# Order of value weighting and high-part subtraction on TensorE in a cross-attention and expert kernel

## The reference

```python
def xattn(q, k, v):
    qh, kh, vh = proj(q, w_q, b_q), proj(k, w_k, b_k), proj(v, w_v, b_v)   # 16 heads of 16
    scores = einsum('bhqd,bhkd->bhqk', qh, kh) / sqrt(16)
    attn = softmax(scores, axis=-1)
    ctx = einsum('bhqk,bhkd->bhqd', attn, vh)
    return einsum('bsd,ed->bse', ctx.reshape(B, S, D), w_o) + b_o

x = x + xattn(layernorm(x), ctx_1024, ctx_1024)
x = x + experts(layernorm(x))      # router, top 2 of 8, silu(x @ gate) * (x @ up) @ down
```

## Time and profile before

| what | value |
|---|---|
| median of 3 runs | 978.39 us (977.79 to 980.58) |
| the profiled execution | 976.2 us |
| its span, first to last instruction | 974.4 us |
| PE busy in the span | 875.0 us, 90% |
| DVE busy | 621.6 us, 64% |
| ACT busy | 468.9 us, 48% |
| POOL busy | 290.0 us, 30% |
| mean granted clock of TensorE | 0.958 |

### The profile page before, as it was taken

One profiled execution on the slowest core, in us unless ns is written; L12 is line 12 of the kernel. 1 busy time (PEld: TensorE's weight loads), 2 busy tenths in 40 slices (PEclk: granted clock), 3 DMA queues, 4 the chain that ended last, 5 costly groups with the idle time before them and its releaser, 6 DMA issues.

```text
span 974.4 us, 32193 instructions
## 1 busy us (share of the span) xinstructions
PE 875.0 (90%) x12208; PEld 781.1 (80%) x12208; DVE 621.6 (64%) x1930; ACT 468.9 (48%) x891; POOL 290.0 (30%) x337
## 2 busy tenths in 40 slices
PE   2899789999999761799999999999999999999995
PEld 1667667777777541789999999999999999999995
DVE  7788858888988544457547447545745746544443
ACT  3677757788878551335335334333523534323321
POOL 5556643344343325012112112212211112211111
PEclk9998979999999775899999999999999999999999
DMA  4321123222224312152522522522332352222221
GB/s 136 112 57 42 60 66 90 67 85 65 89 67 147 104 45 95 51 180 35 162 56 44 152 53 37 160 33 52 103 88 56 66 152 35 33 33 34 33 33 17
DMA packets 69073, 73.57 MB, mean 75 GB/s; under 512 B 19725, under 2 KB 62811, under 8 KB 69019
## 3 DMA queue, kind: packets, MB, share of 16 engines
q1 hardware_dynamic: 44666, 32.94, 11.7%
q0 software_dynamic: 12944, 17.87, 10.7%
q10 hardware_dynamic: 11408, 22.06, 6.4%
HBM read 45.18 MB, written 26.39 MB: 73 GB/s over the span
## 4 chain that ended last, share of the span: by engine, by line
PE 50%; issue 6%; DMA 6%; DVE 3%; ACT 3%; POOL 1%; SPq 0%; POOLq 0%; another core or an unknown queue 0%; ACTq 0%; DVEq 0%
PE bank L483 11%; PE bank L485 11%; PE bank L484 11%; PE bank L681 5%; PE bank L683 5%; PE bank L682 5%; DMA raw<-expert_rows 4%; DMA expert_rows<-rows,slot_u 2%; PE bank L656 1%; POOL expert_rows L1388 1%; PE bank L544 1%; DVE h_full L1252 1%; ACT h_hi L830 1%; DVE h_lo L1258 1%; ACT pt_hi L758 1%
## 5 line engine op out<-in xcount | busy, mean ns | idle before, releaser
L483 PE MATMUL bank<-xg,e_hi 128*128 128x128 f16 x2176 | 372.7, 219 | 0.7 <-DVE xg L1229 0.6
L484 PE MATMUL bank<-xg,e_hi 128*128 128x128 f16 x2176 | 372.7, 219 | 0.0
L485 PE MATMUL bank<-xg,e_lo 128*128 128x128 f16 x2176 | 372.7, 219 | 0.0
L1419 POOL DMA_INDIRECT out<-y_sb,tok_row x68 | 113.4, 1668 | 466.0 <-DVE y_sb L1247 442.5
L483 PEld LDWEIGHTS bank<-xg,e_hi 128*128 128x128 f16 x2176 | 213.4, 98 | 2.0 <-issue 0.8
L484 PEld LDWEIGHTS bank<-xg,e_hi 128*128 128x128 f16 x2176 | 213.4, 98 | 0.8
L485 PEld LDWEIGHTS bank<-xg,e_lo 128*128 128x128 f16 x2176 | 213.4, 98 | 0.0
L828 ACT ACTIVATE g_act<-bank 128x512 f32<-128x512 f32 x136 | 81.3, 598 | 249.1 <-PE bank L485 230.2
L1252 DVE SCALAR_TENSOR_TENSOR h_full<-bank,g_act 128x512 f32<-128x512 f32 x136 | 94.0, 691 | 129.3 <-ACT g_act L828 121.6
L681 PE MATMUL bank<-e_hi,h_hi 128*128 128x256 f16 x544 | 148.4, 273 | 3.8 <-DVE h_lo L1258 3.8
L682 PE MATMUL bank<-e_lo,h_hi 128*128 128x256 f16 x544 | 148.3, 273 | 0.0
(11 more groups left out here) (175 smaller groups left out, 1766.2 us busy)
## 6 DMA issues: line engine op xcount, KB each, us to landing
raw<-expert_rows SPq DMA_DIRECT2D x68, 132.5 KB, 2.6
e_stage<-in_gate_w ACTq DMA_DIRECT2D x7, 1024.0 KB
e_stage<-in_up_w ACTq DMA_DIRECT2D x7, 1024.0 KB
e_stage<-in_down_w ACTq DMA_DIRECT2D x7, 1024.0 KB
expert_rows<-pads SPq DMA_DIRECT2D x8, 530.0 KB
xin<-in_x SPq DMA_DIRECT2D x16, 256.0 KB, 2.8
xres<-in_x SPq DMA_DIRECT2D x16, 256.0 KB
out<-x SPq DMA_DIRECT2D x16, 256.0 KB
```

What stands on the lines that cost most here:

```text
L483: pe.matmul(dst, a_hi(c), b_hi(c), start=c == 0, stop=False)
L484: pe.matmul(dst, a_hi(c), b_lo(c), start=False, stop=False)
L485: mm = pe.matmul(dst, a_lo(c), b_hi(c), start=False, stop=ends and c == chunks - 1)
L1419: pool.indirect_dma_start(out, bass.IndirectOffsetOnAxis(tok_row[:], 0), y_sb[:], None, compute_op=ALU.add).then_inc(added, 16)
```

## The change

In TensorE's `body` two statements change places: `weigh_values` of unit u-2 now comes right behind `score`, and `take_high` of unit u-1 behind it. Nothing else changes: the same instructions, the same waits on the same semaphores, and on ScalarE, VectorE, GpSimd and SyncE the same order.

```diff
                 for u in range(UNITS):
                     if at := unit(c, b, a, u + 2):
                         score(at[0], at[0].plus % 2, at[1])
+                    if at := unit(c, b, a, u - 2):
+                        weigh_values(at[0], at[0].plus % 2, at[1])
                     if (at := unit(c, b, a, u - 1)) and at[1] in LOW_ON_ACT:
                         take_high(*at)
-                    if at := unit(c, b, a, u - 2):
-                        weigh_values(at[0], at[0].plus % 2, at[1])
                     if b:
                         turn_probs(b, u)
```

## The result

The changed kernel takes 973.85 us (median of 10 runs, 971.63 to 976.19) where the kernel before took 978.11 (10 runs, 976.15 to 980.58): a ratio of 0.9956, with a 95% interval of 0.9942 to 0.9970. That is 4.3 us or 0.44% faster. The profiled execution took 971.63 us (span 969.9) beside 976.2 of before.

The account below looks back on a forecast made before the run. The prediction took ScalarE's own order, in a ring with TensorE, as the attention half's bound. Terms -1.2 - 0.3 - 0.3 + 0.8 = -1.0 us gave 975.2 profiled, 977.4 as median; range 974.0 to 981.0.

Parts of the forecast that it names:

- The ring of 1.92 us: Attention steps: TensorE's `take_high` and ScalarE's pt_hi wait for each other; one turn, pt_hi to pt_hi, takes 1.92 us.
- part 5: Step 6: value matmuls waiting for `att` now delay `take_high`, 0.08 us a batch; 0.8 us lost over ten loop batches.
- Rival A: Attention half: if TensorE is the bound, each waited `take_high` gives 0.31 us, 15 us in all; chance 0.17, full form 0.04.
- rival B: Step 6: the wait for `att` delays `take_high` 0.29 us, deciding from 0.2 a batch; 4.6 us slower, 983; chance 0.12.
- Part 1: Steps 6 and 7: value matmuls (0.31 us) fill TensorE's wait ahead of `take_high`; 24 such places, gain 0.
- part 4: Step 4: later `take_high` makes operations slip 0.13 us, covered by idle time before step 6's exponential; no net term.
- price of weight loads: Skill's rule: about 107 ns per 128 columns, so twelve value matmuls take 1.3 us instead of 0.31; the forecast rejected it.
- Part 2: Step 0: pt_hi waits less for transposes, up to 0.31 us at 4 places, 1.2 us; batches outside the stretch 0.3 together.
- Part 3: Batch start to residual: the query projection starts 0.06 us earlier in half the batches; gain 0.3 us, at most 1.0.
- a tie of 0.10 us: Step 6 at full clock: pt_hi starts 0.10 us after the transpose ends, so TensorE is barely behind ScalarE's order.

Follow-up runs that it names:

- before_third: The kernel before, unchanged, measured once more for its trace; no late posts: 973.33 us (one run).
- after_fourth: The changed kernel measured again against the kernel before, without late posts: 969.00 us, ratio 0.9980.
- all_but_6: The changed kernel with step 6 keeping its old order in every batch: 966.72 us, ratio 0.9974 to the kernel before.
- small_before_2: The kernel before with the last three batches' residual stores cut to one of 128 partitions, second measurement: 971.13 us, ratio 0.9995 to the kernel before.
- small_after: The changed kernel with the last three batches' residual stores cut to one of 128 partitions: 965.81 us, ratio 0.9968 to the kernel before.
- loop_only: The kernel before with the new order in the loop of ten bodies alone: 975.71 us, ratio 0.9970.
- after_third: The changed kernel measured again against the kernel before, with late posts: 973.89 us (6 runs), ratio 0.9948.
- all_but_4_6: The changed kernel with steps 4 and 6 keeping the old order: 977.14 us, ratio 0.9984 to the kernel before.
- before_again: The kernel before, unchanged, measured once more for its trace; with late posts: 977.12 us (one run).
- steps_1_7: The kernel before with the new order in steps 1 and 7 alone, in every batch: 976.12 us, ratio 0.9969.
- small_before: The kernel before with the last three batches' residual stores cut to one of 128 partitions, first measurement: 969.52 us, ratio 1.0008 to the kernel before.
- all_but_6_2: The changed kernel with step 6 keeping its old order, measured again: 967.90 us, ratio 0.9962 to the kernel before.
- steps_1_7_2: The kernel before with the new order in steps 1 and 7 alone, measured again, without late posts: 968.36 us, ratio 0.9979.

## Why the prediction was wrong

**What bounds the kernel: right, in the loop.** The ring of 1.92 us stood wherever no late post, no slow stretch and no wait for `att` (part 5) lengthened it. Rival A's full form (0.31 us for each of 24 places) did not come, and neither did rival B: `take_high` starts 0.17 us after pt_hi's end, under the 0.2 from which it decides.

**Part 1: right.** 24 places became 11, and u5 and u6 did not get shorter. The Trainium skill's price of weight loads (TensorE: Matmul & The Clock Gate, section LDWEIGHTS), weighed and set aside in part 4, did not show either: twelve value matmuls take 0.32 us with nothing long ahead of them.

**Part 2: right in place, near in size.** The waits of step 0's pt_hi are nearly gone (0.2 us). The term was 1.2 us over eight batches, 0.15 a batch; without late posts u7 goes from 2.24 to 2.12, 0.12 a batch. With late posts it gives 0.2 to 0.3, since there u7 was 2.35 to 2.44 to begin with.

**Part 3: not seen.** u1 and u2 are unchanged (2.64 and 2.90 to 2.92). In the traces without late posts u0 to u2 together are 0.02 us a batch shorter, 0.2 in ten; that this is the path of part 3 is not shown.

**Part 4: right.** The slip was put at 0.13 and is 0.15, without late posts 0.13. u4 then gives back 0.18, 0.05 us a batch more than the slip, which no term had. The cover was said to be the idle time ahead of the exponential of step 6, and the traces without late posts show it being used up. The time line of ScalarE in steps 3 to 5, before (before_third):

```profile
226.69 0.59 ACT L785 ACTIVATE pt_lo<-bank 77x512 f16<-77x512 f32 x1 [0.48 <-PE bank L551]
227.28 0.46 ACT L752 ACTIVATE probs<-probs 128x308 f32<-128x308 f32 x1
...
229.87 0.46 ACT L752 ACTIVATE probs<-probs 128x308 f32<-128x308 f32 x1 [0.26 <-DVE probs L994]
```

and after (after_fourth):

```profile
226.27 0.59 ACT L785 ACTIVATE pt_lo<-bank 77x512 f16<-77x512 f32 x1 [0.77 <-PE bank L551]
226.76 0.45 ACT L752 ACTIVATE probs<-probs 128x308 f32<-128x308 f32 x1
...
229.13 0.46 ACT L752 ACTIVATE probs<-probs 128x308 f32<-128x308 f32 x1
```

The wait for L551 grew from 0.48 to 0.77, and the 0.26 ahead of the next exponential are gone.

**Part 5: right.** 0.08 us a batch was forecast, 0.09 measured (u5 1.92 to 2.01), and it vanishes when step 6 alone keeps the old order. Of this the batch gets only 0.05: without late posts it takes 19.20 us in the changed kernel and 19.10 and 19.19 in turn in all_but_6.

**The step that failed** is the sentence of part 2, "The batches outside this stretch have other, longer waits behind the same places; I give them 0.3 us together, an estimate of one such place". The drain lies there and gave 2.0 us, 2.4 with late posts. It was costed from no row at all. Three things differ in it, of which the first two could have been read in the trace before:

First, a cover is gone. In step 1 `take_high` waits for pt_hi and the value matmuls of the last unit stand behind it; on them hang the sums, `att`, its transposes (L577) and at_hi. In the loop ScalarE copies xt_hi ahead of at_hi (219.85 and 220.33 in before_third) and the delay is hidden; in the drain there is no next batch, and no xt_hi. The time line of the last batch, before (before_third):

```profile
337.17 0.41 PE L551 MATMUL bank<-pt_hi,minus 77*77 77x512 f16 x1 [0.40 <-ACT pt_hi L758]
...
337.90 0.26 DVE L1005 RECIPROCAL inv_sum<-bank 128x16 f32<-128x16 f32 x1 [0.79 <-PE bank L485]
...
338.68 0.66 PE L577 MATMUL bank<-ident,att 128*128 128x128 f32 x4 [0.32 <-DVE att L1009]
...
339.37 0.60 ACT L764 ACTIVATE at_hi<-bank 128x512 f16<-128x512 f32 x1 [0.33 <-PE bank L577]
```

and after (after_fourth):

```profile
335.55 0.26 DVE L1005 RECIPROCAL inv_sum<-bank 128x16 f32<-128x16 f32 x1
335.63 0.41 PE L551 MATMUL bank<-pt_hi,minus 77*77 77x512 f16 x1
...
336.32 0.66 PE L577 MATMUL bank<-ident,att 128*128 128x128 f32 x4
...
337.40 0.59 ACT L764 ACTIVATE at_hi<-bank 128x512 f16<-128x512 f32 x1
```

Of the three idle times 0.79, 0.32 and 0.33 none is left. Unit 1 to unit 2 falls from 2.37 to 1.92, 0.45 us. With the new order in steps 1 and 7 alone it is 1.92 as well, and with it in the loop alone 2.36: it is step 1, and it is the drain. (In two of the traces with late posts it is 2.08 and 2.15.)

Second, in the last unit TensorE is the bound, and rival A's mechanism holds. Another cover is gone: there is no unit behind it, so ScalarE has no exponential to do ahead of pt_hi, and pt_hi waits for the transposes alone. In three kernels this unit ran at a granted clock of 1.00 throughout. ScalarE's time line with the old order (small_before_2):

```profile
349.37 0.58 ACT L759 ACTIVATE pt_hi<-bank 77x512 f16<-77x512 f32 x1
...
351.29 0.59 ACT L759 ACTIVATE pt_hi<-bank 77x512 f16<-77x512 f32 x1 [0.24 <-PE bank L545]
```

and with the new order in step 7 (all_but_6), pt_lo followed by pt_hi at once:

```profile
347.35 0.58 ACT L761 ACTIVATE pt_hi<-bank 77x512 f16<-77x512 f32 x1
348.43 0.59 ACT L788 ACTIVATE pt_lo<-bank 77x512 f16<-77x512 f32 x1 [0.50 <-PE bank L551]
348.92 0.58 ACT L761 ACTIVATE pt_hi<-bank 77x512 f16<-77x512 f32 x1
```

That is 1.92 and 1.57 us, 0.35 less (small_after has 1.57 too). In the two first traces the unit ran at a granted clock of 0.50, the lower of the two levels (1.2 GHz). The table of stretches of before:

```profile
354.00:357.00 3.00, 2.32 (x25) 1.60 (x23) 1.75 (x17) 1.44 (x3) 0.00 (x0) 0.50 0.00 0
```

its time line of ScalarE:

```profile
354.48 0.59 ACT L758 ACTIVATE pt_hi<-bank 77x512 f16<-77x512 f32 x1 [0.23 <-PE bank L544]
...
357.09 0.59 ACT L758 ACTIVATE pt_hi<-bank 77x512 f16<-77x512 f32 x1 [0.68 <-PE bank L544]
```

the table of stretches of the changed kernel:

```profile
350.00:353.00 3.00, 2.53 (x23) 1.69 (x22) 1.46 (x14) 2.02 (x4) 0.19 (x1) 0.50 0.00 0
```

and its time line of ScalarE:

```profile
350.96 0.58 ACT L758 ACTIVATE pt_hi<-bank 77x512 f16<-77x512 f32 x1
...
353.13 0.59 ACT L758 ACTIVATE pt_hi<-bank 77x512 f16<-77x512 f32 x1 [0.26 <-PE bank L544]
```

The time that pt_hi waits for the transposes goes from 0.68 to 0.26, and the unit from 2.61 to 2.17 us. Where the new order stands in step 7 it was 2.17 to 2.19 in eight traces, where it does not, 2.59 to 2.61 in seven. (In the other five the clock was at 1.00 for all or a part of it.) Averaged over the traces without late posts this unit gives 2.42 - 1.88 = 0.54 us.

Half clock makes TensorE the bound also where the exponential stands. From unit 5 to unit 6 of the last batch ScalarE's time line, old order at a clock of 0.50 (loop_only, whose drain is as before), is:

```profile
351.89 0.59 ACT L761 ACTIVATE pt_hi<-bank 77x512 f16<-77x512 f32 x1 [1.13 <-remote]
...
354.49 0.59 ACT L761 ACTIVATE pt_hi<-bank 77x512 f16<-77x512 f32 x1 [0.33 <-PE bank L544]
```

and with the new order (after_third), at 0.50 from 349.35 on:

```profile
349.18 0.59 ACT L758 ACTIVATE pt_hi<-bank 77x512 f16<-77x512 f32 x1 [0.52 <-issue]
...
351.37 0.59 ACT L758 ACTIVATE pt_hi<-bank 77x512 f16<-77x512 f32 x1
```

2.60 and 2.19 us. All ten traces without late posts have 1.94 or 1.95 here under either order, with the clock at 1.00 until at most the last 0.2 us. So in the traces at hand this counts only with late posts, where the unit falls into the slow stretch, and not always: the trace after has 2.46. The prediction had the number that made both likely, a tie of 0.10 us between the transposes and ScalarE's own order at full clock, and noted that none of its terms held a slow stretch; it should have had one for the drain, where the page's row of the clock shows several.

Third, batch 14: from its unit 2 to its unit 5, 12.2 to 13.0 us in four traces of the old order without late posts and 11.2 to 12.0 in three of the new. The clock is granted at half for different parts of it in each, and with the new order in these steps all_but_6 took 12.3 as well. So the 0.9 us are a difference of averages whose cause is open, and they may be scatter in part.

The three make 0.45 + 0.5 + 0.9 = 1.9 of the 2.0 us, and for 1.0 of it the cause is shown.

**Late posts** were in no step either. With them the account gives 4.4 us instead of 3.0, and so their part in the error is about 1.4 us, 1.0 in the loop and 0.4 in the drain. In the last batch unit 4 to unit 5 takes 3.5 to 4.1 us in the four kernels with the new order in step 4, 4.75 to 4.9 in five with the old order there and 6.05 in a sixth (all_but_4_6): it goes with the order of step 4, and why is open. In batch 14 the new order did not shorten it (4.76 to 5.08).

**The total.** Loop: forecast 1.2 + 0.3 - 0.8 = 0.7 us, got 1.0, 2.0 with late posts. Outside it: forecast 0.3, got 2.0, 2.4 with late posts. The range reached to 974.0 by adding the forecast's own bounds and a part of rival A; no bound was set for the 0.3 us of the batches outside, the only term that rested on no row. Without late posts the 2.4 us measured would lie inside the range, but by the range's reach into rival A and not by its terms: the drain's 2.0 is missing there as well.

## What to carry to other kernels

Cost a reordering of a pipelined body in each of its forms, fill, loop and drain, and at each level of the clock that the profile shows there: what a stage of another batch or the next unit's work hides in the loop, nothing hides where it is left out, and an order that is worth nothing while ScalarE binds can be worth the whole filled wait at the end of the pipeline or at half clock. A term without a row needs bounds as wide as the waits that stand in the part it covers. And measure a per cent or less on more than one chip, each against the kernel before on the same chip.

## What the runs showed of the hardware

**Chips differ by more than the change.** The same kernel before took 978.7, 978.5, 971.4, 970.7 and 969.2 us in the five sets, each on another chip. No chip was measured twice, so that it is the chip and not the time of measuring is not shown. The traces put 5 to 6 us of the difference in the drain (63.8 to 65.3 us against 58.6 to 59.2), another 1 to 2 in seven batches of the loop, and both go with late posts. Between 145 and 302 us the latest signal of the value matmuls comes 0.46 to 0.96 us after the recorded end in six traces with late posts (before, before_again, loop_only, after, after_third, steps_1_7) and 0.02 in four without (before_third, small_before, after_fourth, all_but_6).

**Late posts.** On the slower chips TensorE's signals arrived together long after the recorded ends, at the same place of the last batch. In before it was L600's at +1.42 us, the score's at +1.74 and the value matmuls' at +3.34, while ScalarE's x2t waited 1.21 us. Where they do not occur, the same stretch reads (before_third):

```profile
345.83 0.61 PE L600 MATMUL bank<-ident,rows 128*128 128x128 f16 x8
...
346.09 0.58 ACT L758 ACTIVATE pt_hi<-bank 77x512 f16<-77x512 f32 x1
346.56 1.02 ACT L769 ACTIVATE x2t<-bank 128x1024 f16<-128x1024 f16 x1
```

That TensorE's recorded end is no proof of a finished matmul is also what the Trainium skill says (Perfetto Trace Analysis, section Summary: the profiler window per engine type): the window runs to an estimated end, and the propagation of the semaphore is hidden from it. The traces agree, with up to 3.3 us between the two in this stretch. The medians of all runs differ between the chips as the traces do (978.7 and 969.2). The cause is open: the late posts fall into the time in which the drain's stores, loads and scatters run together, but the same transfers run on the other chips without them.

**The price of a slow stretch.** In all_but_6_2 the granted clock fell to 0.50 for 3.4 us in the middle of the loop, here in the table of stretches. In the 3.9 us before it fell TensorE was busy 3.40.

```profile
191.00:195.00 4.00, 3.75 (x37) 3.11 (x38) 3.56 (x24) 2.31 (x6) 0.97 (x1) 0.61 0.09 34
```

That batch took 20.20 us, where its neighbours took 19.10 and 19.12 and every second batch of this kernel takes 19.20: 1.0 us for 3.4 us at half clock. In steps_1_7_2 it fell for 3.4 us too, after 4.4 us in which TensorE was busy 3.13, and the two units in it took 2.94 and 2.40 us instead of 1.92 each: 1.5 us.
